# A graph layer's prologue: the last rank and sign groups, the last gathered rows and the first edge features in other places

## The reference, cut to what matters

```python
xn = layernorm(x)                                   # x: 1250 x 512, edges: 20000, sorted by dst
r = concat([xn[src], xn[dst], edge_attr]) @ Wr.T + br    # Wr: 512 x 1536
q = (xn @ Wq.T + bq); k = r @ Wk.T + bk; v = r @ Wv.T + bv   # 8 heads of 64
a = einsum('ehd,ehd->eh', q[dst], k) / 8
attn = segment_softmax(a, dst)
out = segment_sum(v * attn, dst) @ Wo.T + bo
gnn = batchnorm(xn + out)
x = x + gnn + linear_attention(xn)
x = x + bitlinear_ffn(layernorm(x))
```

## Time and profile before

| | us |
|---|---|
| median of 3 runs | 1663.91 |
| lowest, highest | 1661.56, 1664.38 |
| the profiled execution | 1663.52 |
| its span, first to last instruction | 1661.8 |
| TensorE busy | 1556.6 (94%) |
| VectorE, ScalarE, GpSimd busy | 1255.0, 1056.4, 737.9 |

### The profile page before, as it was taken

One profiled execution on the slowest core, in us unless ns is written; L12 is line 12 of the kernel. 1 busy time (PEld: TensorE's weight loads), 2 busy tenths in 40 slices (PEclk: granted clock), 3 DMA queues, 4 the chain that ended last, 5 costly groups with the idle time before them and its releaser, 6 DMA issues. The chain is left out here.

```text
span 1661.8 us, 27175 instructions
## 1 busy us (share of the span) xinstructions
PE 1556.6 (94%) x7290; PEld 1195.5 (72%) x7294; DVE 1255.0 (76%) x3184; ACT 1056.4 (64%) x3725; POOL 737.9 (44%) x746
## 2 busy tenths in 40 slices
PE   7998988999999999999999999999999995899985
PEld 6876666777777777777777777777777773678542
DVE  5876644888888888888888888888887885697666
ACT  4793222777777777777777777777777777573144
POOL 1001123555555555555555555555555643451201
PEclk9998999999999999999999999999999997899997
DMA  6564415666666666766666666666666661643001
GB/s 194 184 236 157 183 54 160 217 202 206 203 208 234 212 213 200 249 195 211 234 210 207 205 209 209 211 215 214 214 203 203 201 192 55 196 154 113 1 20 43
DMA packets 130197, 300.30 MB, mean 181 GB/s; under 512 B 29615, under 2 KB 51254, under 8 KB 130048
## 3 DMA queue, kind: packets, MB, share of 16 engines
q0 software_dynamic: 63600, 180.17, 32.3%
q1 hardware_dynamic: 61264, 107.59, 21.4%
q10 hardware_dynamic: 5184, 10.81, 1.7%
HBM read 271.40 MB, written 66.58 MB: 203 GB/s over the span
## 5 line engine op out<-in xcount | busy, mean ns | idle before, releaser
L897 ACT ACTIVATE wv<-vv,expd 128x64 f32<-128x64 f32 x1256 | 316.6, 334 | 2.8
L909 ACT ACTIVATE old<-old,expd 128x64 f32<-128x64 f32 x1256 | 307.7, 333 | 0.0
L841 POOL DMA_INDIRECT merge<-new,put_id x157 | 163.0, 1038 | 272.9 <-DVE new L1072 240.3
L1117 PE MATMUL psK<-M_hi,efT_hi 128*128 128x512 f32 x628 | 253.5, 404 | 6.3 <-ACT efT_hi L867 6.3
L1117 PE MATMUL psV<-M_hi,efT_hi 128*128 128x512 f32 x628 | 255.8, 407 | 0.0
L1118 PE MATMUL psV<-M_lo,efT_hi 128*128 128x512 f32 x628 | 249.4, 397 | 0.0
L1118 PE MATMUL psK<-M_lo,efT_hi 128*128 128x512 f32 x628 | 249.3, 397 | 0.0
L812 POOL DMA_INDIRECT old<-merge,dst_id x157 | 159.3, 1014 | 132.6 <-DMA merge<-new,put_id 106.7
L883 ACT ACTIVATE expd<-diff 128x32 f32<-128x32 f32 (+1 forms) x79 | 18.2, 230 | 294.5 <-DVE diff L1053 294.5
L812 POOL DMA_INDIRECT kv<-kv_table,src_id x157 | 159.4, 1015 | 73.4 <-issue 47.8
L812 POOL DMA_INDIRECT qc<-q_table,dst_id x157 | 156.4, 996 | 53.2 <-issue 46.9
(11 more groups left out here) (258 smaller groups left out, 3336.6 us busy)
## 6 DMA issues: line engine op xcount, KB each, us to landing
efT<-in_ef_turned_dram SPq DMA_DIRECT2D x78, 512.0 KB, 4.9
merge<-empty ACTq DMA_DIRECT2D x4, 2640.0 KB, 9.7
rows<-merge SPq DMA_DIRECT2D x40, 264.0 KB, 3.5
row_block<-dst_rows POOLq DMA_DIRECT2D x13, 768.0 KB, 5.9
dst_line<-dst_rows SPq DMA_DIRECT2D x78, 128.0 KB, 2.7
end_line<-end_rows SPq DMA_DIRECT2D x78, 128.0 KB, 4.1
kv_table<-kv_out SPq DMA_DIRECT2D x10, 512.0 KB, 3.3
raw<-in_L_gnn_Wr_dram SPq DMA_DIRECT2D x12, 256.0 KB, 5.0
```

The lines of the kernel that those rows point to most:

```text
L841: pool.indirect_dma_start(out=merge[2 * (p % 2) + u][:, :], out_offset=bass.IndirectOffsetOnAxis(ap=put_id[:, t:t + 1], axis=0), in_=new[p ...
L897: act.activation(wv[:, u, h * DH:(h + 1) * DH], vv[p % 2][:, u, h * DH:(h + 1) * DH], ACT.Copy, scale=expd[p % 2][:, u, 0, h:h + 1]).then_ ...
L909: act.activation(rows, rows, ACT.Copy, scale=expd[p % 2][:, u, 1, h:h + 1]).then_inc(old_scaled, 1)
L1117: pe.matmul(out[:, :], efT_hi[b][:, u, c, :], Me_hi[:, c, col:col + D], start=c == 0, stop=False)
```

## The change

Three edits, all in the prologue but for the first load of `edges`:

1. Groups 10 to 13: `LATE` is 10, `EARLY` is 120. `rank_group` 10, 11, 12, 13 moves behind `own_scores(t)` of t = 0, 1, 3, 4; `sign_group` 10 to 13 stands ahead of the copies 0, 2, 5 and 9; `load_block(12)` and `load_block(13)` ahead of the cut row stores 2 and 6. The five instructions that make `seg_end` to `put_id` run twice: for tiles 0 to 119 ahead of `evict(1)`, for the others in iteration 5.
2. Cuts 38 and 39, the transposes and the waits for the loop's last additions stand between the eight bank blocks of `fold(2)`'s first round, whose order becomes 0 to 5, 7, 6.
3. `raw` keeps six of its eight slots; slots 2 and 3 are the new buffer `first_ef`, which outlives the prologue and is `efT[0]` of `edges`. SP loads the features of pair 0 into it in the prologue, once slots 2 and 3 are read for the last time, ahead of all `store_nodes`.

```diff
+        LATE = len(groups) - 4
+        EARLY = groups[LATE][0]
+        def slot(k):
+            i = k % SLOTS
+            if i in (2, 3):
+                return first_ef[:, i - 2, :, :].rearrange("p c e -> p (c e)")
+            return raw[:, i if i < 2 else i - 2, :]
 (SyncE)
+            sp.wait_ge(lo_split, split_at(Q0 + 1) + 1)
+            sp.dma_start(first_ef[:, :, :, :], ef[0, :, :, :, :]).then_inc(first_ef_in, 16)
             for t in range(NT):
                 store_nodes(t)
 (GpSimd)
-            for g in range(len(groups)):
+            for g in range(LATE + 2):
                 load_block(g)
             for k, (lo, n) in enumerate(quads):
+                if k == 2:
+                    load_block(LATE + 2)
+                if k == 6:
+                    load_block(LATE + 3)
                 pool.wait_ge(cut_copied, k + 1)
 (TensorE, fold)
+                    order = (0, 1, 2, 3, 4, 5, 7, 6) if part == 2 and rc == 0 else tuple(range(8))
+                    for i in order:
                         ic, side = i // 2, i % 2
+                        if part == 2 and rc == 0:
+                            between_edge_part(i)
+            def between_edge_part(i):
+                if i == 0:
+                    pe.wait_ge(q_added, NT)
+                if i == 1:
+                    pe.wait_ge(kd_added, NT)
+                if i == 3:
+                    cuts(len(quads) - 2)
+                if i == 4:
+                    cuts(len(quads) - 1)
+                if i == 5:
+                    pe.wait_ge(v2_added, NT)
+                if i == 7:
+                    pe.wait_ge(cut_copied, len(quads))
+                    pe.transpose(banks[6][:, 0:P], seg_end[:, 0:P], ident[:, :])
+                    pe.transpose(banks[6][0:ET - P, P:2 * P], seg_end[:, P:ET], ident[:, :]).then_inc(cut_done, 1)
+                if i == 6:
+                    pe.wait_ge(cut_copied, len(quads) + 2)
-            cuts(len(quads) - 2)
-            cuts(len(quads) - 1)
-            pe.wait_ge(cut_copied, len(quads))
-            (the two transposes, the waits for q_added, kd_added, v2_added and cut_copied)
             fold(2)
 (ScalarE)
-            for g in range(NT, len(groups)):
+            for g in range(NT, LATE):
                 sign_group(g)
             evict(1)
...
+                if k in (0, 2, 5, 9):
+                    sign_group(LATE + (0, 2, 5, 9).index(k))
                 act.wait_ge(cut_done, k + 1)
 (VectorE)
-            for g in range(NT, len(groups)):
+            for g in range(NT, LATE):
                 rank_group(g)
+            segment_ends(0, EARLY, 2)
             evict(1)
...
                 own_scores(t)
+                if t in (0, 1, 3, 4):
+                    rank_group(LATE + (0, 1, 3, 4).index(t))
+                if t == 5:
+                    segment_ends(EARLY, ET, 7)
 (edges)
-        efT = two("efT", [P, 2, C, P])
+        efT = [first_ef, sb("efT1", [P, 2, C, P])]
-                sp.dma_start(efT[b][:, 0:n, :, :], ef[p, :, 0:n, :, :]).then_inc(ef_in[b], 16)
+                if p >= 1:
+                    sp.dma_start(efT[b][:, 0:n, :, :], ef[p, :, 0:n, :, :]).then_inc(ef_in[b], 16)
```

More of the change, by code:

```diff
@@ L101, in layer @@
             iota_col = until_edges("iota_col", [P, 1])
-            prologue(nc, x, WqT, bq, Wr, br, WkT, bk, WvT, bv, src_col, dst_col, dst_row, q_table, kv_table, v2_table, merge,
+            first_ef = until_edges("first_ef", [P, 2, C, P])
+            ef_in = [top.enter_context(nc.semaphore(f"ef_in{i}")) for i in range(2)]
+            prologue(nc, ef, ef_in[0], first_ef, x, WqT, bq, Wr, br, WkT, bk, WvT, bv, src_col, dst_col, dst_row, q_table, kv_table, v2_table, merge,
                      dst_rows, end_rows, cut_rows, ident, xT_hi, xT_lo, M_hi, M_lo, src_id, dst_id, put_id, dst_f, rank,
@@ L107, in layer @@
             w_raw = top.enter_context(nc.sbuf_tensor("w_raw", [P, C, 3 * D], F32, side="right"))
-            edges(nc, ef, q_table, kv_table, merge, ident, M_hi, M_lo, dst_rows, end_rows, cut_rows, src_id, dst_id, put_id,
+            edges(nc, ef, ef_in, first_ef, q_table, kv_table, merge, ident, M_hi, M_lo, dst_rows, end_rows, cut_rows, src_id, dst_id, put_id,
                   dst_f, rank, iota_row, iota_col, w_qkv, w_raw, w_in)
@@ L127, in prologue @@
         quads = [(q, min(4, ET - q)) for q in range(0, ET, 4)]
-        raw = sb("raw", [P, SLOTS, D])
+        raw = sb("raw", [P, SLOTS - 2, D])
         W_hi = sb("W_hi", [P, 2, C, D], F32R)
@@ L210, in load @@
                 n = rows.shape[0]
-                sp.dma_start(raw[0:n, k % SLOTS, :], rows).then_inc(raw_in[k % SLOTS], 16)
+                sp.dma_start(slot(k)[0:n, :], rows).then_inc(raw_in[k % SLOTS], 16)
             def store_kv(t):
@@ L316, in fold @@
                             last.then_inc(folded, 1)
-                        elif rc < C - 1 and i == 7:
+                        elif rc < C - 1 and i == order[-1]:
                             last.then_inc(rounds, 1)
@@ L336, in turn @@
                 for c in range(C):
-                    last = pe.transpose(banks[t % 4][:, c * P:(c + 1) * P], raw[:, k % SLOTS, c * P:(c + 1) * P], ident[:, :])
+                    last = pe.transpose(banks[t % 4][:, c * P:(c + 1) * P], slot(k)[:, c * P:(c + 1) * P], ident[:, :])
                 last.then_inc(turned, 1)
@@ L427, in split @@
                 act.wait_ge(raw_in[k % SLOTS], raw_landed(k))
[L428 removed]
+                act.activation(to, slot(k), ACT.Copy).then_inc(hi_split, 1)
             def split_wr(j):
@@ L605, in _, with segment_ends @@
                 split(Q0 + rc, Wq_lo[:, rc, :], Wq_hi[:, rc, :])
-            for g in range(NT, len(groups)):
+            for g in range(NT, LATE):
                 rank_group(g)
[L608 to L617, removed]
+            def segment_ends(a, b, before):
+                dve.wait_ge(signed, b)
+                dve.wait_ge(ranked, b)
+                dve.tensor_scalar(seg_end[:, a:b], signs[:, a:b], -0.5, P / 2 - 1.0, ALU.mult, ALU.add).then_inc(idx_step, 1)
+                dve.wait_ge(idx_step, before + 1)
+                dve.tensor_tensor(is_end[:, a:b], seg_end[:, a:b], rank[:, a:b], ALU.is_equal).then_inc(idx_step, 1)
+                dve.wait_ge(idx_step, before + 2)
+                dve.tensor_copy(is_end16[:, a:b], is_end[:, a:b]).then_inc(idx_step, 1)
+                dve.scalar_tensor_tensor(signs[:, a:b], is_end[:, a:b], -OOB, dst_f[:, a:b], ALU.mult, ALU.add).then_inc(idx_step, 1)
+                dve.wait_ge(idx_step, before + 4)
+                dve.tensor_scalar(put_id[:, a:b], signs[:, a:b], OOB, None, ALU.add).then_inc(idx_step, 1)
+            segment_ends(0, EARLY, 2)
             evict(1)
@@ L678, in _, with edges @@
             evict(2)
-def edges(nc, ef, q_table, kv_table, merge, ident, Me_hi, Me_lo, dst_rows, end_rows, cut_rows, src_id, dst_id, put_id,
+def edges(nc, ef, ef_in, first_ef, q_table, kv_table, merge, ident, Me_hi, Me_lo, dst_rows, end_rows, cut_rows, src_id, dst_id, put_id,
           dst_f, rank, iota_row, iota_col, w_qkv, w_raw, w_in):
@@ L734, in edges @@
         top = psT[:, 2 * H:4 * H].rearrange("p (u h) -> p u h", h=H)
-        ef_in, row_in, cut_in = ([sem(f"{n}{b}") for b in range(2)] for n in ("ef_in", "row_in", "cut_in"))
+        row_in, cut_in = ([sem(f"{n}{b}") for b in range(2)] for n in ("row_in", "cut_in"))
         kv_in, q_in, old_in, put = ([sem(f"{n}{b}") for b in range(2)] for n in ("kv_in", "q_in", "old_in", "put"))
```

15 lines of the change are left out of this document (4 added, 11 removed).

## The result

| | before | after |
|---|---|---|
| median, us (11 runs each, alternating) | 1664.20 | 1659.09 |
| lowest to highest | 1661.56 to 1666.70 | 1656.94 to 1661.13 |
| span of the profiled execution | 1661.8 | 1655.3 |
| ratio, 95% interval | | 0.9968, 0.9960 to 0.9976 |

A forecast was written before the change was run, and what follows sets the result against it. TensorE, busy 94% of the span, was taken as the bound, so only its standstills and the low clock behind them count. Terms -3.8 (loop), -6.0 (seam) and +0.9 (edge features) gave -8.9: 1655.0 us, range 1651 to 1659.

The forecast's parts named there:

- The 37 rank and sign tiles leave the place: Before part 1's eviction: first destination product starts at 121.1, not 129.59; with the low clock gone, cut 0 is 11.2 earlier.
- What it adds: Destination loop: the moved groups' work delays cut 16, which waits 5.6 us, and the clock drops; net sum -3.8 us.
- the walk to cut 16: Destination loop queues followed: third clear at 159.1, add_q(4) at 169.6, cut 16 at 176.4, 6.3 us earlier than before.
- The seam: Last cuts to the end of edge folding: cuts and transposes between folding blocks take 23.7 us, not 29.7; -6.0.
- The first edge features: Edge stage start: early load brings the first sort 1.3 us earlier, but a new 4.4 us wait drops the clock; +0.9.
- (1): Destination loop runs free: tile 2 is stored before the third clear is issued, cut 16 never waits; 1646.8 us, 18%.
- (2): Destination loop: tile 2's store passes beside the clear, cut 16 waits 2 us, the clock stays; 1648.8 us, 8%.
- (3): Destination loop: fourth clear puts segment ends or cut 24 on the path, with another clock fall; 1659.2 us, 10%.
- (4): Destination loop: store and clear fall into step, so clears 2, 3 and 4 each stop TensorE; slower, 1671.2 us, 4%.
- (5): First destination product also waited for something else, the query weights' low parts, so TensorE isn't brought forward; 1663 us, 2%.

The follow-up runs named there:

- the two pairs of runs: Changed kernel against itself with cuts 38, 39, transposes and waits back ahead of fold(2) (ratio 1.0001); first edit alone (0.9989) against changed kernel without early load (0.9957).
- the best kernel: Changed kernel with rank groups 10 to 13 at iterations' ends, blocks 12, 13 loaded later, sign groups 12, 13 later; 1649.17 us, ratio 0.9920 to the kernel before.
- the best two with the early load: Changed kernel with rank groups at iterations' ends, block loads and sign groups 12, 13 later: clears unmoved (ratio 0.9920 to before) or moved too (0.9922).
- the groups last: Changed kernel with rank groups 10 to 13 behind the last one-hots of iterations 0, 1, 3, 4, block 13 and sign group 13 later; ratio 0.9958 to before.
- rank group 10 last: Changed kernel with rank group 10 alone at the end of iteration 0, block 12's load and sign group 12 later; ratio 0.9981 to the kernel before.
- the seam undone: Changed kernel with cuts 38 and 39, the transposes and all waits back in front of fold(2); ratio 1.0001 to the kernel before.
- best kernel, clears moved: The best kernel with the merge-table clears moved out from between copies 1 and 36; ratio 0.9922 to the kernel before.
- the clears moved: Changed kernel with clears 0 and 1 ahead of copy 0, clears 2 and 3 behind the copies of ends_out; ratio 0.9958 to the kernel before.
- without the early load: Changed kernel with the features of pair 0 loaded at the entry of the edge stage again; ratio 0.9957 to the kernel before.

## Why the prediction was half right

The direction held. The median, 1659.09, lies 0.1 us above the forecast's own range (1651 to 1659) and inside the outer one (1645 to 1660), and of the three terms of the sum two came out. The failing one is the first.

**"The 37 rank and sign tiles leave the place": right.** First product 120.97 (121.1 forecast), cut 0 at 129.41 (129.6), full clock behind it, so the gain there is 11.4 us (11.2).

**"What it adds", -3.8 forecast, -1.1 measured at the last cuts: the mis-sized term, and the step that failed is the walk to cut 16.** Its mechanisms were there: ScalarE's sign group 12 ahead of copy 5, the third clear over tile 2's store, rank group 12 ahead of one-hots 16. Tile 0's rows were stored when forecast (137.5 for 137.7). But copy 4 waited 3.8 us for a cut-row store that stood behind the load of block 12, so sign group 12 ended at 148.2 and not at 146.5. By that 1.7 us cut 7 waited 2.4 instead of 0.7, and the clock fell behind it, which the walk didn't have and which cost some 1.6 us. The second clear went out at 147.66 (146.5 forecast), the third at 161.89 (159.1), and it took 11.5 us from it to add_q(4), not 10.5. Cut 16: 180.2 where 176.4 was forecast; its wait was 6.1 (5.6). From cut 16 to the last cuts it took 1.4 us more than before, so the clock there cost 1.4, not 2.5. The traces show these steps; no run moved the load or sign group 12 alone. The run with the groups last, block 12 and sign group 12 later shows the whole size of it, 9.8 us at the start of `fold(2)`.

**"The seam", -6.0: right.** Measured -6.2, and -6.5 and -5.6 by the two pairs of runs. The last folding matmul ends 23.5 us after the last cuts begin (23.7 forecast), with no wait in between.

**"The first edge features", +0.9: right as a sum, with two errors that cancel.** Measured +0.8 (28.1 against 27.3). The sort moved 0.4 us earlier, not 1.3, and the low clock cost 1.2, not 2.2. The new wait is the one that was forecast, 5.3 us for 4.4. A guess for the first error, not tried by itself: in place of pair 0's features those of pairs 1 and 2 now move beside the first gathers (the second is issued at 261.7).

**The rivals.** (1), the loop running free, didn't happen in the changed kernel, but its 1646.8 is near what the best kernel reaches (1649.2 on its chip): the loop runs almost free there, and not because the store passes first (it is issued 0.25 us behind the third clear), but because the groups stand behind the one-hots and nothing holds the copies. (2), the store passing beside the clear, fell: behind clears 2, 3 and 4 the add_q that needed the store started 11.4, 11.5 and 10.4 us after the clear's issue. The 4 us that this rival allowed from store to add_q would have put add_q(4) near 168.3, 5 us too early. It had them as an estimate from the rule of the Trainium skill ("DMA: Bandwidth & Descriptors", "Queues, rings and completion order") that each DMA engine takes packets from the rows with work in turn; how the engines took turns here no run shows. (3) has the time that was measured, 1659.2, but not its mechanism: nothing waited at cut 24, and the loss was at cuts 7 and 16. (4) was to be decided "at the second clear: if it is issued before tile 0 is stored"; it was issued 10 us after. Clears 2, 3 and 4 did each hold add_q (waits of 7.7, 7.9 and 4.2 us), but only the one in front of a rank group and one-hots reached TensorE with more than 0.6 us. (5) fell with the first row.

## What to carry to other kernels

When work is moved into a loop that another engine consumes, put it behind everything of that iteration that someone waits for, and walk every queue that it enters: here the load ahead of small stores on GpSimd and the sign group ahead of small copies on ScalarE made TensorE wait as well as VectorE's order did. With the rank groups behind the one-hots `fold(2)` started 4.4 us earlier than in the changed kernel, and with the load and the sign group out of the copies' way 9.8 us. A load that waits for that work must not stand in a queue ahead of small stores that others wait for. Where an instruction waits for two engines, look up in the code what it waits for, and check that the one named by the view could have been the last. And an early load only helps if what it brings is what ends the wait; here it turned a covered pause of 6.3 us into an exposed one of 5.3.

## What the runs showed of the hardware

The length of a pause didn't decide alone whether the clock fell, and neither did the program. A wait of 2.77 us at the entry of `edges` was followed by full clock (1.00 over six microseconds) in one trace of the changed kernel and in the best two with the early load, but by 0.72 in the second trace of the same changed kernel, and also with the groups last, with rank group 10 last and with the seam undone. Waits of 2.41, 2.29, 2.19 and 2.13 us at cut 7 were followed by 0.72 or 0.73, one of 2.20 us before the transposes (best kernel, clears moved) by 1.00. One of 6.11 us at the entry, with the clears moved, was followed by 0.69. Behind a wait for a sort the matmuls lost 1.2 us in one kernel (5.3 us of waiting) and 2.3 in another (5.6; mark less sort 11.4 against 9.1).

A `q_table` store of 260 KB issued 1.2 to 2.5 us behind a clear of 2640 KB let its add_q start only 9.6 and 10.9 us (before), 11.4 and 11.5 us (after) after the clear's issue. Issued 0.25 us behind one (best kernel) it let it start after 8.5. The 2 KB stores of cut rows, issued by a third engine, took up to 7.1 us where the median is 1.6 (after). Three of ScalarE's four longest waits for them, 5.9, 4.0 and 3.0 us, end 7.0 to 7.5 us behind the issue of clears 2, 3 and 4. The fourth, 3.8 us, is the one at copy 4: there the load of a block (768 KB) was in flight. With such a load issued just ahead two of these stores took 3.6 to 3.9 us in the changed kernel and with the groups last, 1.7 to 3.3 without the early load. The line for `cut_rows`:

```profile
DMA to landing us min/median/max: 1.5/1.6/7.1
```
